# An audio tower on one core: the two-way layer's weights turned in an earlier stage, and two norms of the dispatch moved into the two-way stage

## What is computed

```python
h = tokens(x)                             # seven strided convolutions, 374 tokens of 192 features
h = h + ssm(layernorm(h))                 # a complex diagonal state space
h = h + routed_ffn(layernorm(h))          # 4 experts, each token to its best one
# the two-way layer
xn = layer_norm(layernorm(h), ln_g, ln_b)
xg, z = split(xn @ Wi + bi)
f = scan(conv1d_same(xg, Wf_conv) + bf_conv)
g = flip(scan(conv1d_same(flip(xg), Wb_conv) + bb_conv))
h = h + (f * silu(z) + g * silu(z)) @ Wo + bo + layernorm(h)
# the soft mixture of 64 experts
x = layernorm(h)
logits = x @ phi_n                        # 1024 slots
Xs = softmax_over_tokens(logits).T @ x    # the inputs of the slots
h = h + softmax_over_slots(logits) @ experts(layernorm(Xs))
```

## Time and profile before

| what | value |
|---|---|
| median of 3 runs | 2250.69 us (2245.63 to 2251.97) |
| the profiled execution's own time | 2253.02 us |
| its span, first to last instruction | 2251.2 us |
| PE busy | 2112.5 us, 94% |
| DVE, ACT, POOL busy | 1329.3, 1112.1, 857.5 us |
| mean granted TensorE clock | 0.973 |
| stage 2 in the span | 1640.0 to 1784.6 us |
| stage 3 in the span | 1784.9 to 2019.9 us |

### The profile page before, as it was taken

How to read it: one execution, slowest core, us unless ns; L and a number is a source line. 1 busy time by engine, 2 the same in 40 slices (tenths; PEclk the granted TensorE clock), 3 DMA queues, 4 the chain that set the end, 5 groups by cost and what they waited for, 6 DMA issues and landing times. The chain is left out here.

```text
span 2251.2 us, 40813 instructions
## 1 busy us (share of the span) xinstructions
PE 2112.5 (94%) x14347; PEld 1897.5 (84%) x14347; DVE 1329.3 (59%) x3454; ACT 1112.1 (49%) x2104; POOL 857.5 (38%) x767
## 2 busy tenths in 40 slices
PE   6999999999999999999999999597979889979998
PEld 5889999999999999999999988487956567769998
DVE  5776667667667667667666765333358567652223
ACT  4556655555555555555565554132335366653320
POOL 4445555555565565455455553110143000100100
PEclk9999999999999999999999999699989899989999
DMA  9400000000000000000000020133510011129966
GB/s 270 154 4 4 5 4 4 5 9 4 5 9 4 3 9 4 4 9 4 4 9 4 1 60 10 60 91 107 147 25 21 21 42 56 69 81 320 333 212 246
DMA packets 97333, 137.15 MB, mean 61 GB/s; under 512 B 14036, under 2 KB 77694, under 8 KB 96507
## 3 DMA queue, kind: packets, MB, share of 16 engines
q1 hardware_dynamic: 75146, 105.18, 14.9%
q10 hardware_dynamic: 15664, 18.69, 2.4%
q0 software_dynamic: 6336, 10.85, 1.7%
HBM read 89.14 MB, written 45.50 MB: 60 GB/s over the span
## 5 line engine op out<-in xcount | busy, mean ns | idle before, releaser
L506 POOL TENSOR_TENSOR t_rstd<-t_var,t_minus_half 128x4 f32<-128x4 f32 (+1 forms) x379 | 367.0, 968 | 632.6 <-DVE t_var L426 631.1
L317 PE MATMUL banks<-t_wt,t_l 128*128 128x256 f32 (+1 forms) x2836 | 598.9, 350 | 0.0
L317 PEld LDWEIGHTS banks<-t_wt,t_l 128*128 128x128 f32 x2836 | 510.8, 192 | 52.7
L380 ACT ACTIVATE t_sq<-banks 128x512 f32<-128x512 f32 (+1 forms) x379 | 215.9, 570 | 569.4 <-PE banks L317 567.9
L434 DVE TENSOR_TENSOR t_yn<-banks,t_rstd 128x512 f32<-128x512 f32 (+1 forms) x379 | 249.0, 657 | 368.1 <-POOL t_rstd L506 366.9
L308 PE MATMUL banks<-t_wt,t_l 128*128 128x128 f32 x2836 | 385.5, 278 | 4.3 <-ACT t_l L398 2.9
L308 PEld LDWEIGHTS banks<-t_wt,t_l 128*128 128x128 f32 x2836 | 354.9, 193 | 14.6 <-ACT t_l L398 4.1
L512 POOL TENSOR_TENSOR t_zrstd<-t_zvar,t_minus_half 128x8 f32<-128x8 f32 x188 | 307.6, 1637 | 12.2 <-DVE t_zvar L470 12.2
L414 ACT ACTIVATE t_l<-banks,t_cols 128x512 f32<-128x512 f32 x376 | 286.3, 777 | 27.9 <-PE banks L370 24.4
L398 ACT ACTIVATE t_l<-banks,t_cols 128x512 f32<-128x512 f32 (+1 forms) x381 | 284.8, 747 | 12.7 <-PE banks L330 7.3
L423 DVE TENSOR_REDUCE t_ss<-t_sq 128x4 f32<-128x512 f32 (+1 forms) x379 | 244.7, 646 | 77.6 <-ACT t_sq L380 70.2
(11 more groups left out here) (382 smaller groups left out, 3340.8 us busy)
## 6 DMA issues: line engine op xcount, KB each, us to landing
t_w_rest<-in_w SPq DMA_DIRECT2D x48, 480.0 KB
ect<-t_ECT SPq DMA_DIRECT2D x16, 750.0 KB, 3.2
t_l<-in_w1a SPq DMA_DIRECT2D x27, 384.0 KB, 3.8
sorted_by_expert<-t_h SPq DMA_DIRECT2D x4, 2400.0 KB
routed_by_expert<-t_h SPq DMA_DIRECT2D x4, 2400.0 KB
...
```

Source lines behind the costliest of these rows:

```text
L317: mm = pe.matmul(psY[bank][:, t * C:end * C], src[:, at:at + P], weights[:, C:(1 + end - t) * C], start=False, stop=(t + 1 == n))
L380: act.activation(T["sq"][:, par, 0:n], psY[bank][:, 0:n], ACT.Square).then_inc(S["squared"], 1)
L506: pool.tensor_tensor(T["rstd"][:, par, 0:n], T["var"][:, par, 0:n], T["minus_half"][:, 0:n], ALU.pow)\
```

## The change

The four transposes go from the start of stage 2 to PE's queue in stage 1, between the early routed tiles and the late ones. ACT's three copies follow there, and they write into tiles of the state space (`cosT`, `sinT`, `Cq`) that are no longer read by then. DVE clears the parts of these that need it and sets the bias columns, now 3 columns wide in a tile of their own (`bcol`), behind the last batch's 36 steps and ahead of the last early pieces. `joint_taps` has the same 18 products in another order, with no wait ahead of them; the six for the biases have a stationary operand of 3 columns instead of 128, and write 3 rows. All three products that ACT waits for now end last, and its five copies stand in a row.

The first two norms of the dispatch (`FIRST_NORMS = 2`) go into the last two batches of stage 2, where `stats` and `apply` have nothing to do. So `q` must live through both stages; it gets a tile `tokens` for the whole program, which it shares with buffers of stage 1 (`xs`, `p60`) and of stage 4 (`ye`, `o`). The other changes follow from this: semaphores that are now needed earlier, and one more wait of ACT ahead of its first routed piece.

```diff
@@ -1144,6 +1144,7 @@
...
         if i == 0 and n == 0:
             act.wait_ge(S["loop_over"], 1)
+            act.wait_ge(S["conv_done"], END)
@@ -1258,6 +1259,44 @@
...
+    T1, T2, bcol = T["cosT"][:, 0:320], (T["sinT"][:, 0:320], view(T["Cq"][:, :, :], [[1, 320]])), T["bcol"]
+    def pe_turn_weights(pe):
+        pe.wait_ge(S["row_ready"], B)
+        for n, name in enumerate(("Wib", "Wia")):
+            for i in range(2):
+                mm = pe.transpose(psQ[:, (2 * i + n) * P:(2 * i + n + 1) * P], T[name][:, i, :], T["ident"][:, :])
+        mm.then_inc(S["weights_turned"], 1)
+    def act_turned_weights(act):
+        act.wait_ge(S["weights_turned"], 1)
+        act.wait_ge(S["bias_columns"], 1)
+        act.wait_ge(S["y_ready"], 2 * B)
+        for rows, to, n in ((slice(0, P), T1, 0), (LOW, T2[0], 1), (HIGH, T2[1], 1)):
+            act.activation(view(to[rows, :], [[192, 2], [1, P]]), view(psQ[rows, :], [[P, 2], [1, P]], 2 * P * n), ACT.Copy)\
+                .then_inc(S["weights_copied"], 1)
+    def dve_joint_prepared(dve):
+        dve.wait_ge(S["y_ready"], 2 * B)
+        link = Link(dve, S["joint_link"])
+        dve.memset(T1[:, 128:192], 0.0)
+        dve.memset(T2[0][LOW, 128:192], 0.0)
+        dve.memset(T2[0][HIGH, :], 0.0)
+        dve.memset(T2[1][HIGH, 128:192], 0.0)
+        dve.memset(T2[1][LOW, :], 0.0)
+        link(dve.memset(bcol[:, :, :, :].rearrange("p a k n -> p (a k n)"), 0.0))
+        bi, bi2 = T["lncol"][:, 4:5], T["lncol"][:, 5:6]
+        dve.tensor_scalar(bcol[:, 0, :, 2], view(bi, [[0, 3]]), 1.0, None, ALU.mult)
+        dve.tensor_scalar(bcol[LOW, 1, 0, 2:3], bi2[LOW], 1.0, None, ALU.mult)
+        dve.tensor_scalar(bcol[HIGH, 1, 1:3, 2], view(bi2[HIGH], [[0, 2]]), 1.0, None, ALU.mult)
+        dve.tensor_scalar(bcol[:, 0, 0, 0:1], bi, -1.0, None, ALU.mult)
+        dve.tensor_scalar(bcol[:, 0, 2, 1:2], bi, -1.0, None, ALU.mult)
+        dve.tensor_scalar(bcol[LOW, 1, 0, 0:1], bi2[LOW], -1.0, None, ALU.mult)
+        dve.tensor_scalar(bcol[HIGH, 1, 2, 1:2], bi2[HIGH], -1.0, None, ALU.mult).then_inc(S["bias_columns"], 1)
@@ -1381,6 +1420,7 @@
...
             for place in range(PLACES, FIRST_PLACE + PIECES * EARLY):
                 pe_piece(pe, piece_at(place), 0, EARLY)
+            pe_turn_weights(pe)
             for k in range(PIECES * (ROUTED - EARLY)):
@@ -1418,6 +1458,7 @@
...
             for place in range(PLACES, FIRST_PLACE + PIECES * EARLY):
                 act_piece(act, piece_at(place), 0, EARLY)
+            act_turned_weights(act)
             for k in range(PIECES * (ROUTED - EARLY)):
@@ -1477,6 +1518,7 @@
...
                 dve_chain(dve, B - 1, step)
                 dve_piece(dve, piece_at(CHAIN - LEFT + step), 0, EARLY)
+            dve_joint_prepared(dve)
             for place in range(PLACES, FIRST_PLACE + PIECES * EARLY):
                 dve_piece(dve, piece_at(place), 0, EARLY)
@@ -1522,7 +1564,6 @@
...
     dve.tensor_scalar(T["nvar"][0:TOK, 0:TPB], T["mv"][0:TOK, :, 1], EPS, None, ALU.add).then_inc(S["nvar"], 1)
-    dve.wait_ge(S["nroot"], k + 1)
@@ -1648,7 +1689,19 @@
...
+def dispatch_stats(dve, T, S, b):
+    norm_stats(dve, T, S, Link(dve, S["soft_nlink"], 2, b), b, lambda t: htile(T, b, t), D)
+def dispatch_norm(dve, T, S, b):
+    dve.wait_ge(S["nroot"], b + 1)
+    norm_apply(dve, T, lambda t: htile(T, b, t), lambda t: T["q"][0:TOK, b % 3, t, 0:D]).then_inc(S["q_ready"], 1)
 RETURNS = 1
+FIRST_NORMS = 2
@@ -1665,36 +1718,25 @@
...
-    T1, T2 = T["bu"][:, 0, 0, 0:320], {0: T["bu"][:, 0, 1, 0:320], 1: T["bu"][:, 0, 2, 0:320]}
-    b1, b2 = (view(T["bu"][:, 1, 0, :], [[P, 3], [1, P]], 3 * P * n) for n in range(2))
-    half = {0: 0, 1: 1, 2: 1}
-    pW, pK, pM, pL = ps[0], ps[2:5], ps[5], ps[6]
+    T1, T2, bcol = T["cosT"][:, 0:320], (T["sinT"][:, 0:320], view(T["Cq"][:, :, :], [[1, 320]])), T["bcol"]
+    half, pK, pM, pL = {0: 0, 1: 1, 2: 1}, ps[2:5], ps[5], ps[6]
...
-            def turn_weights():
-                for n, name in enumerate(("Wib", "Wia")):
-                    for i in range(2):
-                        mm = pe.transpose(pW[:, (2 * i + n) * P:(2 * i + n + 1) * P], T[name][:, i, :], T["ident"][:, :])
-                mm.then_inc(S["weights_turned"], 1)
             def joint_taps():
-                pe.wait_ge(S["weights_copied"], 3)
-                pe.wait_ge(S["bias_columns"], 1)
+                o, other = pL[:, 0:3 * P], lambda k: (T["Wcc"] if k == 2 else T["Wcb"])[:, :]
+                pe.matmul(o, T1[:, 0:128], T["Wca"][:, 2, :], start=True, stop=False)
                 for k in range(3):
-                    other, turned = (T["Wcc"] if k == 2 else T["Wcb"])[:, :], T2[half[k]]
+                    pe.matmul(o[0:3, :], bcol[:, 0, k, :], T["Wca"][:, k, :], start=False, stop=False)
+                    pe.matmul(o[0:3, :], bcol[:, 1, k, :], other(k), start=False, stop=False)
+                pe.matmul(o, T2[1][:, 0:128], other(2), start=False, stop=True)
+                for k, at in enumerate((64, 0)):
+                    pe.matmul(pM[:, 0:3 * P], T1[:, at:at + P], T["Wca"][:, k, :], start=(k == 0), stop=False)
+                    pe.matmul(pM[:, 0:3 * P], T2[k][:, at:at + P], other(k), start=False, stop=(k == 1))
+                for k in range(3):
                     pe.matmul(pK[k][:, 0:3 * P], T1[:, 192:320], T["Wca"][:, k, :], start=True, stop=False)
-                    pe.matmul(pK[k][:, 0:3 * P], turned[:, 192:320], other, start=False, stop=True)
-                    for lhs, low in ((T1, b1), (turned, b2)):
-                        rhs = T["Wca"][:, k, :] if low is b1 else other
-                        pe.matmul(pL[:, 0:3 * P], low[:, k, :], rhs, start=(k == 0 and low is b1), stop=False)
-                        if k < 2:
-                            mm = pe.matmul(pM[:, 0:3 * P], lhs[:, slice(64, 192) if k == 0 else slice(0, 128)], rhs,
-                                           start=(k == 0 and low is b1), stop=(k == 1 and low is b2))
-                        else:
-                            mm = pe.matmul(pL[:, 0:3 * P], lhs[:, 0:128], rhs, start=False, stop=(low is b2))
-                    mm.then_inc(S["joint_done"], 1)
+                    pe.matmul(pK[k][:, 0:3 * P], T2[half[k]][:, 192:320], other(k), start=False, stop=True)\
+                        .then_inc(S["joint_done"], 1)
...
                 pe.wait_ge(S["xh_ready"], b + 1)
...
-            turn_weights()
             joint_taps()
             turn(0)
@@ -1758,16 +1799,11 @@
...
             act.activation(three(LOGIT), three(LOGIT), ACT.Exp, scale=-1.0).then_inc(S["sig"], 1)
-            act.wait_ge(S["weights_turned"], 1)
-            act.wait_ge(S["bias_columns"], 1)
-            for rows, dst, n in ((slice(0, P), T1, 0), (LOW, T2[0], 1), (HIGH, T2[1], 1)):
-                act.activation(view(dst[rows, :], [[192, 2], [1, P]]), view(pW[rows, :], [[P, 2], [1, P]], 2 * P * n), ACT.Copy)\
-                    .then_inc(S["weights_copied"], 1)
             for k in range(3):
                 act.wait_ge(S["joint_done"], k + 1)
                 act.activation(T["Wca"][:, k, :], pK[k][:, 0:3 * P], ACT.Copy).then_inc(S["joint_read"], 1)
-                if k >= 1:
-                    act.activation((T["Wcb"] if k == 1 else T["Wcc"])[:, :], (pM if k == 1 else pL)[:, 0:3 * P], ACT.Copy).then_inc(S["joint_read"], 1)
+            act.activation(T["Wcc"][:, :], pL[:, 0:3 * P], ACT.Copy).then_inc(S["joint_read"], 1)
+            act.activation(T["Wcb"][:, :], pM[:, 0:3 * P], ACT.Copy).then_inc(S["joint_read"], 1)
             act.wait_ge(S["pads_zero"], 1)
@@ -1820,6 +1856,9 @@
...
+            pool.memset(T["q"][:, :, :, D:D + 1], 1.0).then_inc(S["ones_ready"], 1)
+            for b in range(FIRST_NORMS):
+                norm_root(pool, T, S, b)
@@ -1871,17 +1910,7 @@
...
-            link = Link(dve, S["joint_link"])
-            link(dve.memset(T["bu"][:, :, :, :].rearrange("p a m n -> p (a m n)"), 0.0))
-            bi, bi2 = T["lncol"][:, 4:5], T["lncol"][:, 5:6]
...
-            dve.tensor_scalar(b1[:, :, 2], view(bi, [[0, 3]]), 1.0, None, ALU.mult)
...
-            dve.tensor_scalar(b2[HIGH, 2, 1:2], bi2[HIGH], -1.0, None, ALU.mult).then_inc(S["bias_columns"], 1)
+            link = Link(dve, S["sig_link"])
             dve.wait_ge(S["sig"], 1)
@@ -1917,6 +1946,8 @@
                 scan(0, slice(0, P), False)
                 if b + 2 < B:
                     stats(b + 2)
+                else:
+                    dispatch_stats(dve, T, S, b + FIRST_NORMS - B)
                 link(scan(1, slice(0, P), True))
@@ -1927,6 +1958,8 @@
...
                 if b + 2 < B:
                     apply(b + 2)
+                else:
+                    dispatch_norm(dve, T, S, b + FIRST_NORMS - B)
                 if b >= 1:
@@ -2198,12 +2231,10 @@
...
-            norm_root(pool, T, S, 0)
-            pool.memset(q[:, :, :, D:D + 1], 1.0).then_inc(S["ones_ready"], 1)
```

(37 more changed lines are left out.)

## The result

The changed kernel took 2238.77 us (median of 7 runs, 2235.14 to 2240.82), the kernel before 2250.18 (7 runs, 2245.63 to 2252.34): ratio 0.9949, 95% interval 0.9939 to 0.9959, or 11.4 us less. The prediction was 2240.7, that is 10.0 us less than the 2250.7 of the runs shown then.

A forecast was written before the change was run, and what follows sets the result against it. PE was taken to bound both the two-way loop and the dispatch, with gains only where it waits. 3.3 + 4.5 + 2.2 = 10.0 us off the median of 2250.7 gave 2240.7, range 2236.0 to 2246.5.

The forecast's parts named there:

- Term 1: Start of the two-way stage: with the joint taps' transposes moved away, the first convolution starts 3.3 us earlier.
- rival B: Two-way stage: PE waits for batch 0's gated product, the gathers take the taps' gain; 6.7 us in all, 2244.0; chance 0.05.
- The cap: Start of the two-way stage: batch 0's tokens, ready at 1653.46, limit the next transposes, whatever the products gain.
- Moved into stage 1: Stage 1: transposes, copies and DVE's preparation cost nothing, lying in idle times; uncovered they would cost 4.5 us.
- Term 2: Start of the dispatch: first norm moved into the seventh batch, so PE's transposes begin 4.5 us earlier.
- Term 3: Dispatch's first step: second norm moved into the eighth batch, so PE's transposes of the maxima start 2.2 us earlier.
- Rival D: Experts' stage: DMAs that don't move with its start swallow the whole gain, no change, 2250.7 us; chance 0.06.
- Rival A: Dispatch's start and taps: shorter idle and half-speed times make the clock give more, 12 to 13 us, 2238; chance 0.18.
- Rival E: Experts' stage: output stores reading ye in its new tile hold up PE, 14 us slower, 2264.7; chance 0.03.

The follow-up runs named there:

- e2_taps: The kernel before with the new tile layout and the joint taps' change alone, both norms left in the dispatch: 2244.06 us, ratio 0.9979 to the kernel before.
- e7_order: The changed kernel with the taps' last step reordered, batch 0's token transposes ahead of the second tap's products: 2238.37 us.
- e8_prep: The changed kernel with one DVE clear of the preparation in stage 1 made 17 times: 2244.18 us, ratio 0.9977 to the kernel before.
- e4_norm1: The changed kernel with FIRST_NORMS = 1, the second norm left in the dispatch's first step: 2241.81 us, ratio 0.996 to the kernel before.
- e10_fill_end: The changed kernel with 24 and 11 unread identity transposes in PE's two idle times ending the two-way loop: 2234.81 us, ratio 0.9934 to the kernel before.
- e1_layout: The kernel before with only the allocations changed, five tiles as views of tokens, no instruction changed: 2249.08 us, ratio 0.9991 to the kernel before.
- e9_ye_first: The kernel before with ye and o allocated ahead of the experts' other tiles, no instruction changed: 2249.11 us, ratio 0.9999 to the kernel before.

## Why the prediction was right, and where it was not

**Term 1, 3.3 us: 3.40.** The 18 products took 14.19 us (14.2 forecast), with 4.92 us at a granted clock of 0.54 (5.0 taken), the three-column products at the full price. e2_taps alone: 3.34. The products ended 3.78 us earlier in the stage, and 0.38 went back behind them, with ACT's third copy (0.5 forecast). B did not change, and PE read batch 0's gated product 1.96 us behind DVE (1.6 forecast): rival B falls. The cap was rightly named; e7_order met it.

**Moved into stage 1, nothing: true for this change, by the wrong reason.** DVE's preparation took from 1543.84 to 1545.84, 2.0 us where 2.1 were estimated, and 0.70 of the 2.67 us of idle time were left; the copy behind it came 2.66 or 2.67 us after the `t_rout` before it in every profile with or without it, e8_prep's apart. The step that failed is "if it were twice as long, the copy behind it would be 1.5 late, still in front of the same 7.19 us". The wait of 7.19 us is no fixed point in time: it begins with the same DVE work that a late copy delays, by way of SP's queue. I named the DMAs that PE waits for, but not what their issue stands behind. At twice the length the kernel would have lost some 1.3 us, 2.0 - 0.70, an estimate from these rows, and more if PE's clock fell as in e8_prep. PE's and ACT's part do lie inside that wait: PE's transposes end at 1555.47 and ACT's copies at 1556.56, and the late tiles start at 1562.55.

**Term 2, 4.5 us: 4.51, of which 0.51 went back.** From PE's first transposes to the first maximum it is 7.97 us, before 7.46. The prediction counted no gain from the clock; it was a small loss. From the first transposes on, PE's half-speed stretch was 6.27 us (1778.83 to 1785.10, at 0.50), before 5.6 (at 0.51). **Term 3, 2.2: 2.26**, and 2.25 by e4_norm1. The stretch from there to the first `shift` was another 0.27 shorter.

**Rival D, a swallowed gain, falls**: the experts' stage starts as much earlier as the first `shift` does, and it did not get longer.

**Rival A, more from the clock, went the other way**: PE's idle time ahead of the dispatch did fall from 5.94 to 1.42 us, but another of 2.91 us stands ahead of the last yB products, and everything from 1775.1 to 1785.1 ran at 0.50. The Trainium skill, TensorE: Matmul & The Clock Gate, Part 1, says that activity releases the throttle. e10_fill_end agrees as far as it goes: with work in both waits the same place ran at 1.00. My rival looked only at the wait next to the stage's start, not at PE's last two waits together. The median, 2238.77, lies nearer to this rival's 2238 than to the forecast's 2240.7; that is chance, since of what it counted on only the 0.27 us came.

**The difference between 10.0 and 11.4 us.** The stretches with the change gave 9.96 in the profile. That the sum came out to 0.04 us is luck in part: term 1 gave 0.1 more than forecast, and the 0.51 lost and the 0.27 gained behind the two waits were not in it. The rest of the 11.4 is within the interval of the ratio (9.2 to 13.7 us), or it comes from the experts' stage, which was shorter in every profile with `tokens`, by 2.5 us in the mean; the layout alone (e1_layout) was 1 to 2 us faster, at the edge of its interval. Rival E looked at this stage, with the wrong sign. The cause stays open: neither e9_ye_first nor any instruction of the change shows it. The weights' queue is busy 73 to 75% of the 16 engines' time there in either group.
